# q and k of later sequences turned by VectorE, natural token order, and stack loads per head group

## The chip, the core and the metric

One Trainium2 chip, one core of it. The time is microseconds (us) on the device, from one launch of the whole program; a kernel's time is the median of its runs. TensorE multiplies matrices, ScalarE applies functions, VectorE and GpSimd work element by element, SyncE's queue (SP) issues nearly all transfers.

## What is computed

One transformer layer in float32 over 8 sequences of 512 tokens, model width 128, 16 heads of 8 dimensions:

```python
x = x + attn(layernorm(x))   # q, k, v = x @ W + b; q, k, v each layer-normed per head (8 dims), scale, bias
                             # scores = q.k / sqrt(8); softmax over 512 keys; out = probs @ v; out @ Wo + bo
x = x + ffn(layernorm(x))    # (silu(x @ wg.T) * (x @ wu.T)) @ wd.T, hidden 384, integer weights / 127
```

## The kernel before

**Turns and units.** The program runs 8 turns, one for each sequence's attention; turns 2 to 5 are a hardware loop, the others are written out. A turn has 16 units, `u` 0 to 15: four heads (a head group, `g = u // 4`) against 128 keys (`kt = u % 4`). In a unit TensorE multiplies scores for four heads (L897, four matmuls on row strips of 32 partitions, from the stacks `kst` and `qst`), ScalarE takes the exponential in two instructions (L771, three heads and then the fourth), and TensorE multiplies the probabilities of the unit before by `v` (L912, `times_v`). The scores of the next unit may be written as soon as the first of the two exponentials is done, since the first three banks of `scores` are single.

**Side pieces.** All other matrix work of the layer is cut into pieces that TensorE does behind `times_v` of a unit. The table `SIDE` says which unit has which piece, and `BANK` which of the two PSUM banks of `side` it writes. In turn i the pieces are: `a_v` (v of sequence i+1), `a_rq` and `a_rk` (the normed q and k of i+1 transposed by TensorE), `b_Wo` (output projection of i-1), `e_q` and `e_k` (q and k of i+2), `b_x2T` (transposes of i-1), `b_g0` to `b_u2` (gate and up products of i-1, three each), `b_d0` and `b_d1` (down product). A piece waits until VectorE has read what its bank held before: `read_out` names the semaphore for each.

**VectorE.** Its instructions stand in one order written by hand in its `turn(i, phase)`: `centred*` (centring with bias out of `side`), `heads_normed` (qk_n), `affined` (scale and bias of q and k, into `qk_f`), `first_part` and `second_part` (q and k split into two float16 parts), `take_sums` (reads out the attention's sum `oacc`, after 8 units each), `divide`, `turn_heads` (onT, for `b_Wo`), `ln2_stats`, `ln2_apply` (x2n, for `b_x2T`), `copy_x2T`, `silu` (ga), `times_up` (hT), `result` (y). An engine works strictly in its order.

**ScalarE** does the exponentials and three tanh in a turn, behind the second exponential of the units in `TANH_AT`. **GpSimd** does in each turn, in this order: `norm_power` of i+2 (ve, rs; it waits for the statistics and for v_c), `v_squares` (v_sq), `residual` (x_bo), `norm_power` of i-1.

**Transfers.** The float16 parts go to a DRAM buffer (`store_parts`) and come back with rows spread out as the stacks, in two halves of two groups each (`load_stack`). For the first sequence, group 0 goes straight from SBUF to SBUF (`own_stack`), group 1 and the second half through DRAM.

## Time and profile before

| | |
|---|---|
| time, median of 3 runs | 330.37 us (330.34 to 330.46) |
| the profiled execution | 330.57 us, its span 328.8 us |
| busy: TensorE, ScalarE, VectorE, GpSimd | 297.1 (90%), 268.8 (82%), 238.7 (73%), 48.5 us (15%) |
| first exponential, last exponential's start | 24.7 us, 308.6 us |
| first exponential of turn 3, of turn 4 | 133.0 us, 168.4 us |
| mean granted TensorE clock | 0.995 |

The span is from the first to the last instruction of the profiled execution. A busy share is an average: it doesn't say who waits for whom in a unit. TensorE's weight loads overlap its matmuls.

### The profile page before, as it was taken

The numbers are of one execution on the slowest core, as the hardware profiler recorded it, in microseconds if no ns is written. First come the engines' busy times: TensorE is split into PE (matmuls) and PEld (weight loads), VectorE is DVE, ScalarE is ACT, GpSimd is POOL, SyncE is SP. The second block draws the span as 40 slices with busy tenths as digits, with TensorE's granted clock in tenths as the row PEclk, the third lists the DMA queues.
The fourth block names the chain that finished last, engine by engine and source line by source line (L and its number), as shares of the span: only waits on it lengthen the run. The fifth ranks groups of instructions, "written<-read, shape, count | busy, mean of one in ns | idle before, by whom it ended". The sixth has DMA issues, their size and how long they took to land.

```text
span 328.8 us, 10326 instructions
## 1 busy us (share of the span) xinstructions
PE 297.1 (90%) x4002; PEld 131.8 (40%) x4002; DVE 238.7 (73%) x631; ACT 268.8 (82%) x300; POOL 48.5 (15%) x93
## 2 busy tenths in 40 slices
PE   7877957899999999999999999999998998789996
PEld 7773311233243424352353325342432332222676
DVE  4998997358887797869786888689774856272365
ACT  4429949999989998889979998999889998999511
POOL 7610200041004100140004100410021010110020
PEclk9999989999999999999999999999999999999999
DMA  6534140210325023401422032302320243000000
GB/s 187 161 112 142 34 160 4 80 54 0 101 96 163 2 78 119 139 20 64 127 87 73 0 119 85 116 0 96 96 99 2 66 130 131 2 0 2 34 3 32
DMA packets 21716, 24.76 MB, mean 75 GB/s; under 512 B 2096, under 2 KB 17712, under 8 KB 21680
## 3 DMA queue, kind: packets, MB, share of 16 engines
q1 hardware_dynamic: 21104, 23.59, 22.7%
q10 hardware_dynamic: 576, 0.69, 0.7%
q8 instruction: 23, 0.38, 0.5%
q14 instruction: 13, 0.11, 0.1%
HBM read 15.36 MB, written 8.65 MB: 73 GB/s over the span
## 4 chain that ended last, share of the span: by engine, by line
PE 48%; ACT 26%; issue 13%; DVE 9%; DMA 2%; POOL 1%; ACTq 1%; SPq 0%; POOLq 0%; DVEq 0%
ACT probs L771 25%; PE oacc L912 19%; PE side L844 14%; PE scores L897 9%; PE side L837 3%; DMA y<-in_x 2%; DVE qk_c L1090 1%; PE scores L998 1%; DVE x2n L1074 1%; ACT th L737 1%; PE scores L798 1%; POOL rs L591 1%; PE side L998 1%; DVE stats L1065 0%; DVE sums_t L1256 0%
## 5 line engine op out<-in xcount | busy, mean ns | idle before, releaser
L771 ACT ACTIVATE probs<-scores 128x1536 f32<-128x1536 f32 (+1 forms) x256 | 248.5, 1025 | 31.4 <-PE scores L897 28.3
L912 PE MATMUL oacc<-probs,vaug 128*32 128x512 f32 x1024 | 137.8, 610 | 9.0 <-DVE sums_t L1256 4.0
L897 PE MATMUL scores<-qst,kst 32*128 32x512 f16 x512 | 50.8, 386 | 13.5 <-ACT probs L771 11.2
L897 PEld LDWEIGHTS scores<-qst,kst 32*128 32x128 f16 x512 | 13.0, 91 | 67.7 <-ACT probs L771 58.3
L912 PEld LDWEIGHTS oacc<-probs,vaug 128*32 128x32 f32 x1024 | 20.4, 108 | 42.9 <-ACT probs L771 32.4
L589 POOL TENSOR_SCALAR ve<-mv 128x4 f32<-128x4 f32 (+1 forms) x17 | 4.0, 235 | 222.2 <-DVE mv L1068 190.9
L844 PE MATMUL side<-x2T_parts,gu_parts 128*32 128x512 f16 x504 | 34.9, 379 | 0.8 <-DVE x2T_parts L1296 0.5
L844 PEld LDWEIGHTS side<-x2T_parts,gu_parts 128*32 128x32 f16 x504 | 14.1, 96 | 32.6 <-issue 18.4
L844 PEld LDWEIGHTS side<-wqkv,xT 128*32 128x32 f32 x736 | 20.9, 110 | 12.5 <-issue 11.5
L844 PE MATMUL side<-wqkv,xT 128*32 128x128 f32 x736 | 24.1, 273 | 0.9 <-DMA xT<-in_xT 0.9
L1302 DVE SCALAR_TENSOR_TENSOR ga<-th,side 128x512 f32<-128x512 f32 x21 | 14.4, 685 | 12.1 <-ACT th L737 12.0
L844 PEld LDWEIGHTS side<-wdT,hT 128*32 128x32 f32 x672 | 18.9, 110 | 8.4 <-issue 6.3
L1309 DVE TENSOR_TENSOR hT<-side,ga 128x512 f32<-128x512 f32 x23 | 15.9, 690 | 7.1 <-PE side L844 6.2
L844 PE MATMUL side<-wdT,hT 128*32 128x128 f32 x672 | 20.9, 273 | 0.0
L798 PE MATMUL scores<-ident 128*128 128x128 f32 x126 | 17.3, 295 | 1.8 <-POOL ident L568 1.8
L1090 DVE SCALAR_TENSOR_TENSOR qk_c<-side,rs,wqkv 128x128 f32<-128x128 f32 x64 | 17.7, 343 | 1.7 <-PE side L844 1.0
L798 PEld LDWEIGHTS scores<-ident 128*128 128x128 f32 x126 | 16.1, 207 | 3.0 <-POOL ident L568 1.8
L591 POOL TENSOR_TENSOR rs<-ve,neg_half 128x4 f32<-128x4 f32 (+1 forms) x17 | 16.9, 997 | 1.4
L1284 DVE TENSOR_TENSOR x<-side,x_bo 128x512 f32<-128x512 f32 x7 | 4.8, 692 | 15.2 <-PE side L844 15.2
L1247 DVE TENSOR_TENSOR vaug<-v_c,hy 128x128 f32<-128x128 f32 x32 | 7.9, 287 | 9.4 <-PE oacc L912 9.3
L1074 DVE TENSOR_SCALAR x2n<-x,mv,rs 128x128 f32<-128x128 f32 x32 | 10.0, 371 | 5.1 <-POOL rs L591 5.0
L737 ACT ACTIVATE th<-side 128x512 f32<-128x512 f32 x21 | 12.6, 602 | 0.7
(161 smaller groups left out, 291.0 us busy)
## 6 DMA issues: line engine op xcount, KB each, us to landing
parts_dram<-parts SPq DMA_DIRECT2D x16, 256.0 KB, 2.5
qst<-parts_dram SPq DMA_DIRECT2D x15, 256.0 KB, 2.7
kst<-parts_dram SPq DMA_DIRECT2D x15, 256.0 KB, 3.1
x_res<-in_x SPq DMA_DIRECT2D x8, 256.0 KB, 3.5
parts_dram<-parts SPq DMA_DIRECT2D x16, 128.0 KB, 1.9
x_in<-in_x SPq DMA_DIRECT2D x7, 256.0 KB, 2.6
xT<-in_xT SPq DMA_DIRECT2D x7, 256.0 KB, 3.1
out_dram<-y SPq DMA_DIRECT2D x7, 256.0 KB, 2.1
```

The costliest lines, as they stand in the source:

```text
L591: pool.tensor_tensor(out=rs[:, ts], in0=ve[:, ts], in1=neg_half[:, ts], op=ALU.pow).then_inc(rs_done, 1)
L737: act.activation(th[:, j, :], gate, ACT.Tanh, scale=0.5 * GU_SCALE).then_inc(tanh_done, 1)
L771: act.activation(out, src, ACT.Exp).then_inc(exp_done, 1)
L798: pe.matmul(out, ident[:, :], ident[:, :], start=True, stop=True)
L837: last = pe.transpose(dst[:, k * P:(k + 1) * P], src(t), ident[:, :])
L844: last = pe.matmul(out[cols, :], weights[:, cols], moving, start=start, stop=stop)
L897: last = pe.matmul(scores[:, j if j < TRIPLE else TRIPLE + u % 2, :], kst[r, g, kt * P:(kt + 1) * P], qst[r, g, :], start=True, stop=True)
L912: last = pe.matmul(oacc[STRIP * j:STRIP * (j + 1), :], vaug[:, kt, NG * g + j, :], probs[:, kt, j, :], start=first, stop=last_of_half)
L1074: dve.tensor_scalar(dst[:, t, :], src[:, t, :], mv[:, t, 0:1], rs[:, t:t + 1], ALU.subtract, ALU.mult).then_inc(done, 1)
L1090: last = dve.scalar_tensor_tensor(out=out[:, t, :], in0=bank[:, t * D:(t + 1) * D], scalar=rs1[:, t:t + 1], in1=wqkv[:, bias, :], op0=ALU. ...
L1302: dve.scalar_tensor_tensor(out=ga[:, j, :], in0=th[:, j, :], scalar=1.0, in1=gate, op0=ALU.add, op1=ALU.mult)\
L1309: dve.tensor_tensor(out=hT[:, j, :], in0=up, in1=ga[:, j, :], op=ALU.mult)\
```

## The change

q and k of sequences 1 to 7 are no longer transposed by TensorE into PSUM: VectorE transposes 32x32 blocks from SBUF to SBUF (`turned`, into `qk_t`, written with a step of four elements) and `affined` reads that. Sequence 0 keeps TensorE's transposes. `a_rq` and `a_rk` leave the table, and the other pieces move to other units and banks; `b_g1` and `b_g2` share unit 11. Columns of q and k now stand in natural token order; the keys of a unit are therefore every fourth column of `kst`, and rows of the residual and the output are read and written as 512-byte pieces. Each stack load takes one group, in pieces of 256 bytes. All four groups of sequence 0 go from SBUF to SBUF. VectorE's order and `TANH_AT` change.

```diff
-SIDE = {0: ["a_v"], 1: ["a_rq"], 3: ["a_rk"], 4: ["b_Wo"], 5: ["e_q"], 6: ["e_k"], 7: ["b_x2T"],
-        8: ["b_g0"], 9: ["b_u0"], 10: ["b_g1"], 11: ["b_u1"], 12: ["b_g2"], 13: ["b_u2"], 14: ["b_d0"], 15: ["b_d1"]}
-BANK = {"a_v": 1, "a_rq": 0, "a_rk": 1, "b_Wo": 0, "e_q": 1, "e_k": 0, "b_x2T": 1, "b_g0": 1, "b_u0": 0, "b_g1": 1,
-        "b_g2": 1, "b_u1": 0, "b_u2": 0, "b_d0": 0}
-FIRST_SIDE = {1: ["a_v"], 5: ["a_rq"], 6: ["a_rk"], 7: ["e_q"], 8: ["e_k"]}
+SIDE = {0: ["a_v"], 3: ["b_Wo"], 4: ["e_q"], 5: ["e_k"], 6: ["b_x2T"], 9: ["b_g0"], 10: ["b_u0"], 11: ["b_g1",
+        "b_g2"], 12: ["b_u1"], 13: ["b_u2"], 14: ["b_d0"], 15: ["b_d1"]}
+BANK = {"a_v": 1, "b_Wo": 1, "e_q": 0, "e_k": 1, "b_x2T": 0, "b_g0": 1, "b_u0": 0, "b_g1": 1, "b_g2": 0,
+        "b_u1": 1, "b_u2": 1, "b_d0": 1}
+FIRST_SIDE = {1: ["a_v"], 7: ["e_q"], 8: ["e_k"]}
...
-                        eng.dma_start(stack[r:P:SLOTS, 0, :], parts[0:STRIP, part, which, :]).then_inc(group_loaded, 16)
+                        src = parts[STRIP * group:STRIP * (group + 1), part, which, :]
+                        eng.dma_start(stack[r:P:SLOTS, group, :], src).then_inc(loaded, 16)
...
-                for which, stack in ((0, qst), (1, kst)):
-                    src = parts_d[which].rearrange("(c q) r s -> (q r) c s", c=NG)
-                    sp.dma_start(stack[:, 2 * half:2 * half + 2, :], src[:, 2 * half:2 * half + 2, :])\
-                      .then_inc(loaded, 16)
+                for g in (2 * half, 2 * half + 1):
+                    for which, stack in ((0, qst), (1, kst)):
+                        src = parts_d[which].rearrange("a i s n c -> (i s) a n c")
+                        sp.dma_start(stack[:, g, :].rearrange("p (a c) -> p a c", c=P), src[:, :, g, :]).then_inc(loaded, 16)
...
+            for group in range(1, NG):
+                for part in range(2):
+                    for which, stack in ((0, qst), (1, kst)):
+                        own_stack(sp, which, part, stack, group, second_group_loaded if group == 1 else other_groups_loaded)
...
-            TANH_AT = {8: 0, 10: 1, 12: 2}
+            TANH_AT = {9: 0, 11: 1, 12: 2}
...
-                    last = pe.matmul(scores[:, j if j < TRIPLE else TRIPLE + u % 2, :], kst[r, g, kt * P:(kt + 1) * P],
+                    keys = kst[r, g, :].rearrange("p (c t) -> p t c", t=NT)
+                    last = pe.matmul(scores[:, j if j < TRIPLE else TRIPLE + u % 2, :], keys[:, kt, :],
...
+            def turned(b, w):
+                dve.wait_ge(qkn_done, 2 * b + w + 1)
+                at_least(dve, qkf_done, 2 * (b - 1) + w + 1)
+                dve.transpose(qk_t[:, w, :, :, :].rearrange("p n k t -> p n t k"), qk_n[:, w, :, :].rearrange("p t (n i) -> p n t i", i=STRIP))\
+                   .then_inc(qkt_done, 1)
+
             def affined(b, w):
-                dve.wait_ge(r_filled, 2 * b + w + 1)
+                dve.wait_ge(qkt_done, 2 * (b - 1) + w + 1)
                 sc, bi = ((q_aff[:, 0:1], q_aff[:, 1:2]), (k_aff[:, 0:1], k_aff[:, 1:2]))[w]
-                dve.tensor_scalar(qk_f[:, w, :], side[:, BANK[name], :], sc, bi, ALU.mult, ALU.add).then_inc(qkf_done, 1)
+                dve.tensor_scalar(qk_f[:, w, :], qk_t[:, w, :, :, :].rearrange("p n k t -> p (n k t)"), sc, bi,
+                                  ALU.mult, ALU.add).then_inc(qkf_done, 1)
...
             def first_part(b):
-                at_least(dve, parts_stored, 16 * PART_DMAS * b)
                 if isinstance(b, int) and b == 1:
                     dve.wait_ge(group_loaded, 16 * GROUP_DMAS)
+                    dve.wait_ge(second_group_loaded, 16 * OWN_DMAS)
+                    dve.wait_ge(other_groups_loaded, 32 * OWN_DMAS)
+                else:
+                    dve.wait_ge(parts_stored, 16 * PART_DMAS * (b - 1))
...
                     heads_normed(1)
-                    fill_v(0, 1)
-                    centred_v(1)
-                    ln1_stats(2)
+                    turned(1, 0)
+                    turned(1, 1)
                     affined(1, 0)
                     affined(1, 1)
                     first_part(1)
                     second_part(1)
+                    fill_v(0, 1)
+                    centred_v(1)
+                    ln1_stats(2)
+                    take_sums(0, 0)
                     centred(2, 0)
...
                     centred(2, 1)
                     later_square(2, 0)
                     later_square(2, 1)
-                    sums_v(1)
-                    take_sums(0, 0)
-                    divide(0, 0)
```

Three places in the instruction order of a turn follow, where the table and VectorE's order decide it.

TensorE, units 9 to 11 of turn 1 before: each gate or up product is 12 matmuls of L844 on `x2T_parts`, between a unit's `times_v` (L912) and the next unit's scores (L897).

```order
L844 MATMUL side<-x2T_parts,gu_parts 32x512 x12
L897 MATMUL scores<-qst,kst 128x512 x4
L912 MATMUL oacc<-probs,vaug 32x512 x4
L844 MATMUL side<-x2T_parts,gu_parts 32x512 x12
L897 MATMUL scores<-qst,kst 128x512 x4
```

The same place in the changed kernel, units 10 to 12 (there L839, L893 and L908 are the same lines):

```order
L839 MATMUL side<-x2T_parts,gu_parts 32x512 x12
L893 MATMUL scores<-qst,kst 128x512 x4
L908 MATMUL oacc<-probs,vaug 32x512 x4
L839 MATMUL side<-x2T_parts,gu_parts 32x512 x24
L893 MATMUL scores<-qst,kst 128x512 x4
L908 MATMUL oacc<-probs,vaug 32x512 x4
L839 MATMUL side<-x2T_parts,gu_parts 32x512 x12
```

Unit 11 now holds 24 matmuls in place of 12, and units 7 and 8 hold none.

VectorE, late in turn 1 before: `ga` is `silu` and `hT` is `times_up`, here of gates 1 and 2 (the last rows are the start of the head norm's inverse roots).

```order
L1302 SCALAR_TENSOR_TENSOR ga<-th,side 128x512
L1309 TENSOR_TENSOR hT<-side,ga 128x512
L1136 TENSOR_REDUCE qk_sum<-qk_sq 128x128
L1139 TENSOR_SCALAR hv<-qk_sum 128x128
L1302 SCALAR_TENSOR_TENSOR ga<-th,side 128x512
L1309 TENSOR_TENSOR hT<-side,ga 128x512
L1149 TENSOR_SCALAR hy<-hv 128x192
```

The same place in the changed kernel, from `times_up` of gate 0 on:

```order
L1319 TENSOR_TENSOR hT<-side,ga 128x512
L1136 TENSOR_REDUCE qk_sum<-qk_sq 128x128
L1139 TENSOR_SCALAR hv<-qk_sum 128x128
L1312 SCALAR_TENSOR_TENSOR ga<-th,side 128x512
L1274 RECIPROCAL rinv<-sums_t 128x32
L1278 TENSOR_TENSOR on_t<-sums_t,rinv 128x16x16
L1312 SCALAR_TENSOR_TENSOR ga<-th,side 128x512
L1319 TENSOR_TENSOR hT<-side,ga 128x512 x2
L1149 TENSOR_SCALAR hy<-hv 128x192
```

`times_up` of gate 1 has moved behind `silu` of gate 2, and `divide` of this turn's first half stands between the two `silu`.

VectorE at the start of turn 1 before:

```order
L1247 TENSOR_TENSOR vaug<-v_c,hy 128x4x4x8 x2
L1256 STREAM_TRANSPOSE sums_t<-oacc 128x512
L1090 SCALAR_TENSOR_TENSOR v_c<-side,rs,wqkv 128x128 x4
L1264 RECIPROCAL rinv<-sums_t 128x32
L1268 TENSOR_TENSOR on_t<-sums_t,rinv 128x16x16
L1065 BN_STATS stats<-x_in 128x6 x4
L1068 BN_AGGR mv<-stats 128x2 x4
L1205 TENSOR_SCALAR qk_f<-side,q_aff 128x512
L1278 STREAM_TRANSPOSE onT<-on_t 128x512
```

and in the changed kernel:

```order
L1065 BN_STATS stats<-x_in 128x6 x4
L1068 BN_AGGR mv<-stats 128x2 x4
L1266 STREAM_TRANSPOSE sums_t<-oacc 128x512
L1257 TENSOR_TENSOR vaug<-v_c,hy 128x4x4x8 x2
L1090 SCALAR_TENSOR_TENSOR v_c<-side,rs,wqkv 128x128 x4
L1204 STREAM_TRANSPOSE qk_t<-qk_n 128x4x4x32
L1210 TENSOR_SCALAR qk_f<-qk_t,q_aff 128x512
L1274 RECIPROCAL rinv<-sums_t 128x32
L1278 TENSOR_TENSOR on_t<-sums_t,rinv 128x16x16
L1288 STREAM_TRANSPOSE onT<-on_t 128x512
```

The statistics of the next x stand first now, and the new transpose and `affined` stand between v_c and the two instructions of `divide`.

## Rows read from the trace of the kernel before

**Rows 1.** Group of instructions: line, engine, names, count | busy us, mean ns | idle before:

```profile
L897 PEld LDWEIGHTS scores<-qst,kst 32*128 32x128 f16 x512 | 13.0, 91 | 67.7 <-ACT probs L771 58.3 <-issue 9.4
```

**Rows 2.** Timeline, turn 3, TensorE's scores: start, us, engine, line, [idle before, releaser]:

```profile
136.82 0.39 PE L897 MATMUL scores<-qst,kst 32*128 32x512 f16 x4
...
138.77 0.40 PE L897 MATMUL scores<-qst,kst 32*128 32x512 f16 x4 [0.47 <-ACT probs L771]
...
140.84 0.40 PE L897 MATMUL scores<-qst,kst 32*128 32x512 f16 x4
...
149.41 0.40 PE L897 MATMUL scores<-qst,kst 32*128 32x512 f16 x4
...
151.81 0.39 PE L897 MATMUL scores<-qst,kst 32*128 32x512 f16 x4
...
158.18 0.40 PE L897 MATMUL scores<-qst,kst 32*128 32x512 f16 x4
...
162.44 0.39 PE L897 MATMUL scores<-qst,kst 32*128 32x512 f16 x4
...
165.24 0.39 PE L897 MATMUL scores<-qst,kst 32*128 32x512 f16 x4
...
168.00 0.40 PE L897 MATMUL scores<-qst,kst 32*128 32x512 f16 x4
```

**Rows 3.** Timeline, the second half of turn 3:

```profile
151.04 0.83 PE L844 MATMUL side<-x2T_parts,gu_parts 128*32 128x512 f16 x12
...
152.13 1.07 PE L912 MATMUL oacc<-probs,vaug 128*32 128x512 f32 x8
...
161.08 0.69 DVE L1302 SCALAR_TENSOR_TENSOR ga<-th,side 128x512 f32<-128x512 f32 x1 [0.87 <-ACT th L737]
...
162.93 1.07 PE L912 MATMUL oacc<-probs,vaug 128*32 128x512 f32 x8
```

**Rows 4.** Timeline, VectorE and GpSimd early in turns 3 and 4:

```profile
136.86 0.87 DVE L1065 BATCH_NORM_STATS2 stats<-x_in 128x6 f32<-128x128 f32 x4
...
138.09 0.81 DVE L1205 TENSOR_SCALAR qk_f<-side,q_aff 128x512 f32<-128x512 f32 x1
...
138.44 0.23 POOL L589 TENSOR_SCALAR ve<-mv 128x4 f32<-128x4 f32 x1 [27.06 <-DVE mv L1068]
...
138.81 0.70 DVE L1278 STREAM_TRANSPOSE onT<-on_t 128x512 f32<-128x512 f32 x1
...
139.75 1.04 POOL L595 TENSOR_TENSOR v_sq<-v_c 128x512 f32<-128x512 f32 x1
...
168.01 0.69 DVE L1315 TENSOR_TENSOR y<-side,x 128x512 f32<-128x512 f32 x1 [0.39 <-PE side L844]
...
170.50 1.13 DVE L1090 SCALAR_TENSOR_TENSOR v_c<-side,rs,wqkv 128x128 f32<-128x128 f32 x4
...
171.55 0.35 DVE L1264 RECIPROCAL rinv<-sums_t 128x32 f32<-128x32 f32 x1
...
171.93 0.43 DVE L1268 TENSOR_TENSOR on_t<-sums_t,rinv 128x256 f32<-128x256 f32 x1
```

**Rows 5.** Timeline, the same two engines early in turn 6:

```profile
242.28 1.04 POOL L595 TENSOR_TENSOR v_sq<-v_c 128x512 f32<-128x512 f32 x1 [24.77 <-DVE v_c L1090]
...
242.50 1.11 DVE L1268 TENSOR_TENSOR on_t<-sums_t,rinv 128x256 f32<-128x256 f32 x1
```

**Rows 6.** Timeline, turn 0, with SyncE's queue (SPq):

```profile
19.01 2.30 SPq L421 DMA_DIRECT2D qst<-parts  x3
...
34.00 1.29 DVE L1196 TENSOR_TENSOR qk_n<-qk_c,hy 128x512 f32<-128x512 f32 x2
...
41.29 1.22 DVE L1233 TENSOR_TENSOR parts<-qk_f,parts 128x1024 f16<-128x1024 f32 x1
...
47.38 1.91 PE L912 MATMUL oacc<-probs,vaug 128*32 128x512 f32 x8 [3.66 <-DVE sums_t L1256]
...
49.94 13.47 ACT L771 ACTIVATE probs<-scores 128x1536 f32<-128x1536 f32 x13 [4.17 <-PE scores L897]
```

More of the change, by code:

```diff
@@ L69 @@
 WARM_LAST = {"on": 8, "x2n": 11, "x2T": 3}
[L70 removed]
+STACK_DMAS = NG
 W_KS = ([0], [1, 2])
@@ L130, in occupants_before @@
     if phase == "first":
-        p, turn = [(p, turn) for p, turn in PROLOGUE if same_bank(p) and (p, sequence_of(p, turn)) not in ELSEWHERE][-1]
+        p, turn = [(p, turn) for p, turn in PROLOGUE
+                   if (p, sequence_of(p, turn)) not in ELSEWHERE and same_bank(p)][-1]
         return [(p, sequence_of(p, turn))]
@@ L410, in build, with own_stack @@
         GROUP_DMAS = 2 * SLOTS
-        def own_stack(eng, which, part, stack):
+        OWN_DMAS = 2 * (SLOTS - 1)
+        def own_stack(eng, which, part, stack, group, loaded):
             if which == 0:
@@ L522, in _ @@
             for part in range(2):
-                own_stack(sp, 0, part, qst)
-            for part in range(2):
-                for which in range(2):
-                    own_store(sp, which, part)
-            for which, stack in ((0, qst), (1, kst)):
-                load_second_group(sp, which, stack)
+                own_stack(sp, 0, part, qst, 0, group_loaded)
+            for group in range(1, NG):
+                for part in range(2):
+                    for which, stack in ((0, qst), (1, kst)):
+                        own_stack(sp, which, part, stack, group, second_group_loaded if group == 1 else other_groups_loaded)
+            sp.wait_ge(shift_stored, 32)
             sp.wait_ge(flag_ready, 1)
@@ L1398, in turn @@
                     return
-                fill_v(i, 1)
+                if early:
+                    ln1_stats(i + 2)
                 if behind:
                     take_sums(i - 1, 1)
+                fill_v(i, 1)
                 if ahead:
                     centred_v(i + 1)
+                    turned(i + 1, 0)
+                    affined(i + 1, 0)
                 if behind:
                     divide(i - 1, 1)
-                if early:
-                    ln1_stats(i + 2)
+                    turn_heads(i - 1)
+                    ln2_stats(i - 1)
                 if ahead:
-                    affined(i + 1, 0)
-                if behind:
-                    turn_heads(i - 1)
-                if ahead:
-                    affined(i + 1, 1)
-                if behind:
-                    ln2_stats(i - 1)
+                    turned(i + 1, 1)
                 if early:
@@ L1419, in turn @@
                     ln2_apply(i - 1)
+                if ahead:
+                    affined(i + 1, 1)
+                if early:
+                    later_square(i + 2, 0)
+                if ahead:
+                    sums_v(i + 1)
                 if early:
@@ L1425, in turn @@
                 if early:
-                    later_square(i + 2, 0)
+                    later_square(i + 2, 1)
+                if behind:
+                    silu(i - 1, 0, side[:, BANK["b_g0"], :])
                 if ahead:
                     first_part(i + 1)
-                divide(i, 0)
-                if ahead:
-                    sums_v(i + 1)
-                if behind:
-                    silu(i - 1, 0, side[:, BANK["b_g0"], :])
-                if early:
-                    later_square(i + 2, 1)
+                    second_part(i + 1)
                 if behind:
                     times_up(i - 1, 0, side[:, BANK["b_u0"], :])
-                if ahead:
-                    second_part(i + 1)
-                if behind:
-                    silu(i - 1, 1, side[:, BANK["b_g1"], :])
-                    times_up(i - 1, 1, side[:, BANK["b_u1"], :])
                 if early:
@@ L1445, in turn @@
                 if behind:
+                    silu(i - 1, 1, side[:, BANK["b_g1"], :])
+                divide(i, 0)
+                if behind:
                     silu(i - 1, 2, side[:, BANK["b_g2"], :])
+                    times_up(i - 1, 1, side[:, BANK["b_u1"], :])
                     times_up(i - 1, 2, side[:, BANK["b_u2"], :])
@@ L1457, in turn @@
                     result(i - 1)
-                if ahead:
-                    fill_v(i + 1, 0)
             turn(0, "first")
```

101 lines of the change are left out of this document (51 added, 50 removed).

## The prediction

> **What bounds the kernel now.** I read the page first: TensorE is busy 90%, ScalarE 82%, VectorE 73%, and none is full, so I looked at one turn of the loop in the timeline, by the starts of its scores [rows 2]. Call s0 to s15 the starts of a turn's sixteen scores; a unit lasts from one to the next. Turn 3 gives: a unit without a side piece 138.77 - 136.82 = 1.95 (unit 2); with four full transposes of q or k 2.07 (unit 3); units 4 to 7 with Wo, e_q, e_k and x2T 8.57 together; unit 8 2.40; units 9 to 13, one gate or up product each, 162.44 - 151.81 = 10.63, so 2.13 each; unit 14, with half a down product, 2.80, and unit 15 2.76. The reader is to see two regimes: in a plain unit TensorE waits for ScalarE (the idle time named in the row of 138.77), and the two exponentials set 1.95; in a unit with a float32 piece TensorE itself is the longer. Every 0.1 us that TensorE starts a unit's scores late is lost for both. Unit 8 is 2.40 because its product waited for x2T_parts: the product starts at 151.04 [rows 3], 1.63 after the unit's start, where otherwise a piece follows the scores by 0.32 and 1.07 of `times_v` [rows 3]. Turn 0 has one large hole: `times_v` of unit 8 waits 3.66 us for `take_sums` on VectorE, and ScalarE stands idle 4.17 us [rows 6].
>
> **Turn 0: a gain of about 4.1.** `take_sums(0, 0)` moves ahead of the centring of sequence 2, its squares and sums_v. What stays ahead of it is what VectorE did from 34.00 to 42.51 [rows 6] (qk_n's start to the end of the second part), plus two block transposes at 0.70 [rows 4] (that of onT). The transposes put its start at 43.9 at worst, and at about 42.3 if the waits in that stretch go (`affined` no longer waits for TensorE, and the first of `parts` doesn't meet v_sq any more, below). It takes about 0.7, and `times_v` wants it at 47.38 - 3.66 = 43.72. So the hole shrinks by 3.3 to 4.2; I take 4.1. `first_part(1)` now also waits until 18 more small transfers have read `parts`: three took the queue 2.30 [rows 6], so 18 at most 13.8, issued by 35.1, landed before 38, when VectorE gets there. xT of sequence 2, queued behind them, has until unit 7 at about 40.
>
> **Transposes off TensorE: -0.2 a turn.** Two units lose theirs. One was worth 2.07 - 1.95 = 0.12; the other stood behind a longer unit and I take 0.07.
>
> **x2T earlier: -0.45 a turn.** x2T is now in unit 6 and the first product in unit 9, so 2.40 becomes 1.95, provided VectorE has copied x2T by then. By my count of its order it has, with over 1 us to spare.
>
> **Two products in unit 11: +0.67 a turn.** A product is busy 0.83 [rows 3]; directly behind another part of its filling is hidden, so I take 0.67 (bounds 0.6 and 0.83): unit 11 becomes 2.80. Five product units become four plus this.
>
> **The new wait, for u2: +0.85 a turn.** Both u1 and u2 write bank 1, so u2 waits until `times_up` has read u1, and in VectorE's order that stands behind `silu` of gate 2, which waits for the tanh at the end of unit 12. Before, this `silu` started at 161.08 [rows 3], 2.90 after s12 at 158.18 [rows 2]. It takes 0.69, `times_up` about the same again, and with 0.1 for the signal u2 starts at s12 + 4.4 at the latest and 4.3 at the earliest. From a product's start to the next scores is 151.81 - 151.04 = 0.77, so s14 comes at s12 + 5.1 where it was 162.44 - 158.18 = 4.26: +0.85. Unit 14 gives 0.17 back: its `times_v` had to wait for the exponentials (162.93 - 162.44 = 0.49 against 152.13 - 151.81 = 0.32 [rows 2, 3]) and won't. So the late part of the turn costs 0.67 + 0.85 - 0.17 = +1.35, the early part gives 0.64: **+0.7 a turn**, in seven turns (the last has the same second half) **+5.0**. The same chain then runs on: the inverse roots, `fill_v` and `heads_normed` now all stand ahead of `result`, so y starts about 0.3 later than 168.01 [rows 4].
>
> **The start of the turn: 0 to +0.6 in six turns.** Measured from s0 (168.00 in turn 4). y at 0.3, to the next instruction 0.6; the statistics 138.09 - 136.86 = 1.23 [rows 4]; sums and vaug 1.05; so v_c starts at 3.2 and ends at 4.3. The transpose 0.70; `affined` reads SBUF now: no row has it at this shape, from PSUM it took 0.81 [rows 4], half of that is the lower bound, I take 0.5. The reciprocal 171.93 - 171.55 = 0.38, so on_t starts at about 5.9. GpSimd meanwhile waits for v_c, since the statistics are early: ve at 4.4, and v_sq 139.75 - 138.44 = 1.31 later [rows 4], 5.7 to 6.75. In turn 6 on_t started 0.22 after v_sq, took 1.11 in place of 0.43 and ended 0.29 after v_sq's end [rows 4, 5]. The same here would end on_t at 7.05, onT at 7.8, and Wo starts at 7.9. TensorE would start it at 7.3: unit 0 at 2.2 (a_v is a piece like Wo, e_q and e_k: 8.57 less about 2.0 for x2T, over three), two plain units 3.9, then 1.2 for scores and `times_v`. So Wo and all behind it come 0.6 late: 3.6 in turns 1 to 6. If on_t slips in before v_sq, it costs nothing (onT at 7.1). The two are 0.2 apart on a sum of eight terms, so I take half, **+1.8**.
>
> **The keys' step and the block transposes' step.** The weight loads of the scores take 91 ns [rows 1] and stand in the chain from one exponential to the next in plain units. No row shows one with a step; I take no change, bounded above by doubling, 0.09 in each of 128 units, 11.6. The new transpose writes with a step of 16 bytes; lower bound 0.70, upper twice that. The second case is cheap: ahead of on_t it hides in the hold above, ahead of x2T's copy in the spare time, about 1.5 in all. In the page "SBUF — State Buffer", section "Door 1: The DMA port swizzle", the Trainium skill says that accesses reach full bandwidth with at least two hits on a 16-byte line. By that rule the keys, 8 bytes apart, load as before, and the transposes' writes, each in a new line, would be dearer, which speaks against this change; no row here compares the two.
>
> **Transfers: 0.** A stack half is now four transfers. The parts are stored earlier than before, and the loads were issued at the end of a turn with a quarter of a turn to spare. The 512-byte pieces of the residual and the output are hidden the same way, except the last store, 0.1.
>
> **Sum.** -4.1 + 5.0 + 1.8 = +2.7, on the profiled execution's 330.57, which stands 0.2 over the median: 333.3 there, **333.1** for the median of the runs.
>
> **The rivals.** (1) *The forecast* holds with on_t between free and always held: 331.3 to 334.9. 0.52. (2) *Faster*: the wait for u2 isn't paid. It would need u1 read out before u2's turn; the place is VectorE between `silu` of gates 1 and 2, and it decides if the tanh of gate 2 ran more than about 0.8 earlier against s12 than in the rows. Then units 12 to 14 are as before, unit 11's 0.67 and the early gain cancel, turns keep their length, and turn 0's gain stands alone: 330.37 - 4.1 = 326.3. For it speaks that I lay out an order by hand, against it that tanh stands behind the second exponential in both. 0.28, with all smaller mixtures that end below 329.7. (3) *Weight loads with a step*: half the bound is +5.8 on the forecast, 338.9; the point from which it decides is 0.02 a unit. 0.10. (4) *Turn 0's hole only moves*: the first parts or a slow transpose keep `take_sums` late and 2 of the 4.1 are lost: 335.1. 0.10.
>
> **How the numbers follow.** A measurement of this kernel can tell about 0.2%, 0.66 us, from no change. Faster is rival 2, and a little of the forecast's lower edge: 0.30. Same, 329.7 to 331.0, lies between rival 2 and the forecast with on_t free: 0.13. The rest is slower: 0.57. The range, 326.2 to 336.5, holds the forecast, most of rival 2 and rival 4; the forecast's own range is 331.3 to 334.9.
>
> **What would show it.** In the changed kernel: in turn 0 TensorE's wait for sums_t under 1 us; plain units still at 1.95 (if not, the weight loads); unit 11 at 2.80; in unit 13 a TensorE wait of about 0.9 for VectorE's hT, each turn; on_t at 1.1 rather than 0.43 beside v_sq, and Wo's piece late by half a microsecond; turns of 36.1 to 36.7, from first exponential to first exponential, where turn 3 had 168.4 - 133.0 = 35.4. The prediction is wrong if u2 finds its bank free, or if some piece that I count as in time (x2T, a_v behind y, `times_v` of unit 8) is late.

## The result and the profile after

The changed kernel takes **341.17 us** (340.95 to 341.37, 4 runs) where the kernel before took 330.36 beside it: ratio 1.0326, 95% interval 1.0304 to 1.0347. It is slower, as forecast, but by 10.8 us where the forecast said 2.7, and it lies outside the range. The line numbers of the changed kernel are 4 or 5 lower on TensorE and ScalarE, those of VectorE from L1204 on 10 higher: scores L893, `times_v` L908, side pieces L839, exponentials L766.

The page, beside the table of before: TensorE's busy time fell by 4.8 us although the span grew by 10.7.

```profile
span 339.5 us, 10249 instructions
...
PE 292.3 (86%) x3946; PEld 127.4 (38%) x3946; DVE 252.4 (74%) x645; ACT 270.0 (80%) x300; POOL 49.3 (15%) x93
```

Turn 3 in the timeline, TensorE's scores, as in [rows 2] (start, us, engine, line):

```profile
134.88 0.41 PE L893 MATMUL scores<-qst,kst 32*128 32x512 f16 x4
...
137.27 0.41 PE L893 MATMUL scores<-qst,kst 32*128 32x512 f16 x4
...
139.23 0.41 PE L893 MATMUL scores<-qst,kst 32*128 32x512 f16 x4
...
141.19 0.41 PE L893 MATMUL scores<-qst,kst 32*128 32x512 f16 x4 [0.41 <-ACT probs L766]
...
144.36 0.41 PE L893 MATMUL scores<-qst,kst 32*128 32x512 f16 x4
...
161.76 0.41 PE L893 MATMUL scores<-qst,kst 32*128 32x512 f16 x4
...
166.78 0.41 PE L893 MATMUL scores<-qst,kst 32*128 32x512 f16 x4
...
169.43 0.41 PE L893 MATMUL scores<-qst,kst 32*128 32x512 f16 x4
...
172.17 0.41 PE L893 MATMUL scores<-qst,kst 32*128 32x512 f16 x4
```

A turn now has 172.17 - 134.88 = 37.3 us where it had 35.4. Unit by unit, from one start to the next:

```
turn 3, unit   0    1    2    3    4    5    6    7    8    9    10   11   12   13   14   15
before        2.20 2.02 1.94 2.07 2.23 2.20 2.20 1.95 2.40 2.11 2.13 2.13 2.13 2.13 2.80 2.76
after         2.38 1.96 1.96 3.17 2.22 2.21 1.96 1.96 1.97 2.21 2.10 2.78 1.99 3.03 2.65 2.73
```

The last seven units are 17.49 against 16.19, so +1.30, and unit 3 alone is 1.10 longer. All turns together, from the starts of their first scores (the last one to its last exponential):

```
turn      0      1      2      3      4      5      6      7
before  37.18  35.77  35.37  35.39  35.35  35.26  35.37  35.19
after   33.95  37.16  38.83  37.28  37.31  37.20  36.81  36.26
```

Turn 0 gives 3.23, the others lose 1.1 to 2.0 each and turn 2 loses 3.46; with 0.65 more ahead of the first scores that makes 10.6 of the span's 10.7. Two questions stood open after this view: what makes unit 3 so long (the forecast had 2.2 or 2.8 there), and what is special in turn 2.

VectorE and GpSimd early in turn 3, with TensorE's Wo piece behind them (these answer to [rows 4, 5]; L1204 is the new transpose, L1278 on_t, L1288 onT):

```profile
139.44 1.25 DVE L1204 STREAM_TRANSPOSE qk_t<-qk_n 128x512 f32<-128x512 f32 x1
...
140.72 0.55 DVE L1210 TENSOR_SCALAR qk_f<-qk_t,q_aff 128x512 f32<-128x512 f32 x1
...
141.03 1.13 POOL L591 TENSOR_TENSOR v_sq<-v_c 128x512 f32<-128x512 f32 x1
...
141.57 0.88 DVE L1278 TENSOR_TENSOR on_t<-sums_t,rinv 128x256 f32<-128x256 f32 x1
...
142.48 0.71 DVE L1288 STREAM_TRANSPOSE onT<-on_t 128x512 f32<-128x512 f32 x1
...
143.34 1.08 PE L839 MATMUL side<-wo,onT 128*32 128x128 f32 x32 [0.60 <-DVE onT L1288]
```

The reader is to see two things. The transpose takes 1.25 us where onT, of the same shape and without a step, takes 0.71. And on_t takes 0.88, ending 0.29 after v_sq's end (142.45 against 142.16), which is the forecast's mechanism to the hundredth. TensorE waits 0.60 for onT. In turns 1 to 5 it is on_t that is held so, in turn 6 `affined` (1.59).

The late part of the turn, VectorE's silu and times_up with TensorE's products (as [rows 3]):

```profile
160.35 1.48 PE L839 MATMUL side<-x2T_parts,gu_parts 128*32 128x512 f16 x24
...
164.68 0.69 DVE L1312 SCALAR_TENSOR_TENSOR ga<-th,side 128x512 f32<-128x512 f32 x1 [1.20 <-ACT th L733]
165.28 0.68 DVE L1319 TENSOR_TENSOR hT<-side,ga 128x512 f32<-128x512 f32 x1
...
166.02 0.83 PE L839 MATMUL side<-x2T_parts,gu_parts 128*32 128x512 f16 x12 [0.75 <-DVE hT L1319]
```

The two products of unit 11 take 1.48, and the product u2 waits 0.75 for hT, behind a ga that waits 1.20 for the third tanh. And turn 2, where VectorE stands still 1.51 us inside the four aggregations of the statistics, with nothing in the profile that it waits for ("issue"):

```profile
97.82 0.23 DVE L1068 BATCH_NORM_AGGREGATE mv<-stats 128x2 f32<-128x6 f32 x2
...
99.56 0.40 DVE L1068 BATCH_NORM_AGGREGATE mv<-stats 128x2 f32<-128x6 f32 x2 [1.51 <-issue]
...
100.78 1.06 PE L908 MATMUL oacc<-probs,vaug 128*32 128x512 f32 x8 [1.98 <-ACT probs L766]
```

This is the first pass through the hardware loop's body. In the kernel before `fill_v` and `take_sums` stood first in a turn; now the statistics do, and `take_sums`, which frees the place that `times_v` of unit 1 writes, is queued behind the stall. `take_sums` ends at 100.73, and `times_v` starts at 100.78; the exponential that the last row names had been done before.

### The profile page after: what moved, and what is told of

It is laid out like the page before. It is cut to its first block and busy times, and to the rows that moved or that the text cites. A ratio compares the mean times of both kernels' runs of the same rounds, so it can differ in the third digit from the quotient of the medians.

```text
span 339.5 us, 10249 instructions
## 1 busy us (share of the span) xinstructions
PE 292.3 (86%) x3946; PEld 127.4 (38%) x3946; DVE 252.4 (74%) x645; ACT 270.0 (80%) x300; POOL 49.3 (15%) x93
## 5 line engine op out<-in xcount | busy, mean ns | idle before, releaser
L766 ACT ACTIVATE probs<-scores 128x1536 f32<-128x1536 f32 (+1 forms) x256 | 248.4, 1024 | 41.5 <-PE scores L893 38.6
L908 PE MATMUL oacc<-probs,vaug 128*32 128x512 f32 x1024 | 136.3, 604 | 8.0 <-ACT probs L766 2.1
L893 PE MATMUL scores<-qst,kst 32*128 32x512 f16 x512 | 52.8, 402 | 21.7 <-ACT probs L766 20.9
L893 PEld LDWEIGHTS scores<-qst,kst 32*128 32x128 f16 x512 | 15.3, 108 | 87.4 <-ACT probs L766 76.2
L839 PE MATMUL side<-x2T_parts,gu_parts 128*32 128x512 f16 x504 | 33.6, 380 | 5.2 <-DVE hT L1319 5.2
L908 PEld LDWEIGHTS oacc<-probs,vaug 128*32 128x32 f32 x1024 | 20.2, 108 | 41.6 <-ACT probs L766 27.0
L839 PEld LDWEIGHTS side<-x2T_parts,gu_parts 128*32 128x32 f16 x504 | 13.7, 96 | 34.5 <-issue 13.2
L839 PEld LDWEIGHTS side<-wqkv,xT 128*32 128x32 f32 x736 | 20.2, 110 | 13.9 <-issue 11.0
L839 PE MATMUL side<-wqkv,xT 128*32 128x128 f32 x736 | 24.1, 273 | 1.0 <-DVE qk_c L1090 0.6
L839 PEld LDWEIGHTS side<-wdT,hT 128*32 128x32 f32 x672 | 19.0, 110 | 8.3 <-issue 4.8
L839 PE MATMUL side<-wdT,hT 128*32 128x128 f32 x672 | 20.9, 273 | 0.0
L793 PE MATMUL scores<-ident 128*128 128x128 f32 x126 | 18.6, 309 | 1.8 <-POOL ident L564 1.8
L1266 DVE STREAM_TRANSPOSE sums_t<-oacc 128x512 f32<-128x512 f32 (+1 forms) x17 | 11.6, 683 | 10.4 <-PE oacc L908 10.2
L793 PEld LDWEIGHTS scores<-ident 128*128 128x128 f32 x126 | 17.6, 224 | 3.0 <-POOL ident L564 1.8
L587 POOL TENSOR_TENSOR rs<-ve,neg_half 128x4 f32<-128x4 f32 (+1 forms) x17 | 18.0, 1058 | 1.4
L1204 DVE STREAM_TRANSPOSE qk_t<-qk_n 128x512 f32<-128x512 f32 x14 | 16.5, 1193 | 0.0
L598 POOL TENSOR_TENSOR x_bo<-x_res,bo_row 128x512 f32<-128x512 f32 x8 | 11.1, 1390 | 22.1 <-DMA x_res<-in_x 22.1
```

The lines of the kernel that those rows point to most:

```text
L587: pool.tensor_tensor(out=rs[:, ts], in0=ve[:, ts], in1=neg_half[:, ts], op=ALU.pow).then_inc(rs_done, 1)
L598: pool.tensor_tensor(out=x_bo[:, :, :], in0=x_res[:, :, :], in1=bo2_row[:, :].unsqueeze(1).broadcast_to((P, NT, D)), op=ALU.add)\
L766: act.activation(out, src, ACT.Exp).then_inc(exp_done, 1)
L793: pe.matmul(out, ident[:, :], ident[:, :], start=True, stop=True)
L839: last = pe.matmul(out[cols, :], weights[:, cols], moving, start=start, stop=stop)
L893: last = pe.matmul(scores[:, j if j < TRIPLE else TRIPLE + u % 2, :], keys[:, kt, :], qst[r, g, :], start=True, stop=True)
```

## The experiments

Each edit is made in the changed kernel unless it says otherwise. "Less" is the difference of the medians to the changed kernel's 341.17. The kernel before, which ran beside every one of them, moved by up to 0.5 between these occasions (329.99 to 330.48), so the ratios are the better measure: by them experiments 1, 2, 5 and 7 gave 4.3, 4.4, 1.0 and 7.6.

**1. times_up of gate 1 ahead of silu of gate 2.** Theory: the new wait for u2 comes from this order alone.

```diff
-                    silu(i - 1, 2, side[:, BANK["b_g2"], :])
                     times_up(i - 1, 1, side[:, BANK["b_u1"], :])
+                    silu(i - 1, 2, side[:, BANK["b_g2"], :])
```

> The changed kernel with one edit: on VectorE times_up of gate 1 stands ahead of silu of gate 2, as before the change. Theory (the wait for u2 costs what it shows): the trace of the changed kernel has s12 to s14 at 1.99 + 3.03 = 5.02 in turn 3 where it was 4.26, so units 12 and 13 should fall to about 4.25, unit 14 rise by about 0.15, net 0.6 to 0.8 in each of seven turns: 336.0 to 337.0 from 341.2. Rival (the wait hides a later one, such as the down product waiting for hT of gate 2): TensorE's wait moves to unit 14 and the time stays within 1 us of 341.2.

336.56 us, ratio 1.0196 (1.0178 to 1.0215): 4.6 less. Turn 3, TensorE and VectorE around unit 13:

```profile
162.02 0.69 DVE L1319 TENSOR_TENSOR hT<-side,ga 128x512 f32<-128x512 f32 x1 [0.39 <-PE side L839]
...
162.83 0.69 DVE L1312 SCALAR_TENSOR_TENSOR ga<-th,side 128x512 f32<-128x512 f32 x1
163.25 0.83 PE L839 MATMUL side<-x2T_parts,gu_parts 128*32 128x512 f16 x12
```

hT now stands ahead of ga and u2 starts with no wait beyond its place; unit 13 is 2.29 instead of 3.03, unit 14 2.80 instead of 2.65. The wait for u2 and what it costs are shown: 4.1 in units 13 and 14 of seven turns. Another 0.45 went in unit 0, since y is no longer late (in turn 3 it starts 0.03 after the turn's first scores, where it was 0.35).

**2. The transpose written without a step.** This changes the order of the output's columns, so part of what is computed is not the reference's; the work is the same.

```diff
-    dve.transpose(qk_t[:, w, :, :, :].rearrange("p n k t -> p n t k"), ...)
+    dve.transpose(qk_t[:, w, :, :, :].rearrange("p n k t -> p (n k t)")
+                  .rearrange("p (n t k) -> p n t k", t=NT, k=STRIP), ...)
```

> The changed kernel with VectorE's transposes written without a step, so that the columns of q and k of sequences 1 to 7 come out in another order (the output is not the reference's). Theory A (the step of 16 bytes makes a transpose dear): 1.2 us falls to 0.70. Theory B (at the turn's start on_t is held by GpSimd's v_sq in any case, so the dearer transpose is hidden there): Wo's piece comes as late as before within 0.1, and the time falls by less than 1 us, 340.2 to 341.2. If the transpose itself makes Wo late, the time falls by 0.5 in six turns, to about 338.2.

336.19 us, ratio 1.0192 (1.0162 to 1.0223): 5.0 less. Groups of instructions of this kernel and then the same two of the changed one (busy us, mean ns):

```profile
L1204 DVE STREAM_TRANSPOSE qk_t<-qk_n 128x512 f32<-128x512 f32 x14 | 9.8, 703 | 0.0
...
L1278 DVE TENSOR_TENSOR on_t<-sums_t,rinv 128x256 f32<-128x256 f32 (+1 forms) x17 | 7.6, 450 | 0.6
```

```profile
L1204 DVE STREAM_TRANSPOSE qk_t<-qk_n 128x512 f32<-128x512 f32 x14 | 16.5, 1193 | 0.0
...
L1278 DVE TENSOR_TENSOR on_t<-sums_t,rinv 128x256 f32<-128x256 f32 (+1 forms) x17 | 9.7, 569 | 0.6
```

Its timeline in turn 3:

```profile
139.08 0.42 DVE L1278 TENSOR_TENSOR on_t<-sums_t,rinv 128x256 f32<-128x256 f32 x1
139.09 1.31 POOL L591 TENSOR_TENSOR v_sq<-v_c 128x512 f32<-128x512 f32 x1
...
139.54 0.71 DVE L1288 STREAM_TRANSPOSE onT<-on_t 128x512 f32<-128x512 f32 x1
```

The step costs 0.49 us of VectorE for each transpose. But the second effect is as large: on_t starts 6.13 after the turn's first scores where it was 6.69, and v_sq stays (6.14, it was 6.15). So on_t starts 0.01 ahead of v_sq, takes 0.42, and it is GpSimd that is held (1.31). Unit 3 falls to 2.36 in every turn, 4.3 in turns 1 to 6 together. So the dear transpose and the hold don't overlap, they add: the one causes the other.

**3. GpSimd's order turned round.** x_bo first in a turn, as soon as its data is there, v_sq last, behind both `norm_power`.

```diff
+                if "b" in PHASES[phase]:
+                    residual(i - 1)
                 ...
-                if "a" in PHASES[phase]:
-                    v_squares(i + 1)
                 ...
-                    residual(i - 1)
+                if "a" in PHASES[phase]:
+                    v_squares(i + 1)
```

> The changed kernel with GpSimd's order in a turn changed: x_bo first, then norm_power of i+2, norm_power of i-1, and v_sq last, so that nothing long of GpSimd runs beside on_t. Theory (the hold): on_t falls from 0.88 to 0.43 in turn 3 and Wo's piece comes 0.45 earlier in turns 1 to 6, minus what x2n loses beside v_sq, up to 0.4: 338.5 to 341.0. Rival (the hold is a coincidence of the record): on_t stays at 0.88 and the time at 341.2.

342.35 us, ratio 1.0377 (1.0355 to 1.0399): slower. The timeline shows where the hold went (L1171 is the last step of the inverse roots, hy):

```profile
131.48 1.35 POOL L598 TENSOR_TENSOR x_bo<-x_res,bo_row 128x512 f32<-128x512 f32 x1 [21.16 <-DMA x_res<-in_x]
...
131.72 1.33 DVE L1171 SCALAR_TENSOR_TENSOR hy<-ht,hy 128x192 f32<-128x192 f32 x1
...
135.79 1.08 PE L840 MATMUL side<-wqkv,xT 128*32 128x128 f32 x32 [0.91 <-DVE y L1326]
```

on_t takes 0.42 again and unit 3 fell to 2.68 to 2.87 in the loop, but now hy, which takes 0.36 alone, is held to 1.33 beside x_bo, y comes late, and the piece a_v waits 0.91 for y: unit 0 grows from 2.3 to 3.3. A hold that is moved needs a place where VectorE has time.

**4. The heads turned before q.** `turned` and `affined` of q behind `turn_heads`.

```diff
-                    turned(i + 1, 0)
-                    affined(i + 1, 0)
                 if behind:
                     divide(i - 1, 1)
                     turn_heads(i - 1)
-                    ln2_stats(i - 1)
+                if ahead:
+                    turned(i + 1, 0)
+                    affined(i + 1, 0)
+                if behind:
+                    ln2_stats(i - 1)
```

> The changed kernel with the first turned and affined of a turn behind turn_heads, so that divide and turn_heads follow v_c at once, as before the change. Theory (late onT makes unit 3 long): unit 3 falls from 3.17 to 2.2 in turns 2 to 5 and less in 1 and 6; 5.0 us in all, 336 to 337. Rival (the work ahead of x2T's copy is the next to be late): half of it comes back as a wait for x2T_parts or sums_t at units 8 and 9, 338 to 340.

337.50 us, ratio 1.0216 (1.0195 to 1.0238): 3.7 less. Timeline, turn 3:

```profile
140.51 1.03 POOL L591 TENSOR_TENSOR v_sq<-v_c 128x512 f32<-128x512 f32 x1
...
141.47 1.61 DVE L1210 TENSOR_SCALAR qk_f<-qk_t,q_aff 128x512 f32<-128x512 f32 x1
141.51 1.28 POOL L598 TENSOR_TENSOR x_bo<-x_res,bo_row 128x512 f32<-128x512 f32 x1
```

Unit 3 is 2.36. The hold now falls on `affined`, 1.61 in place of 0.55, ending 0.29 after x_bo's end, where nobody waits. The gain stays under experiment 2's 5.0 because turn 2 lost more: its unit 1 grew from 3.39 to 4.10.

**5. The keys side by side.** `kst` read without the step of four; a unit's probabilities then meet the rows of v of other keys, so the attention is not the reference's; the work is the same.

```diff
-                    keys = kst[r, g, :].rearrange("p (c t) -> p t c", t=NT)
+                    keys = kst[r, g, :].rearrange("p (t c) -> p t c", t=NT)
```

> The changed kernel with each unit's keys taken as 128 adjacent columns of kst again, so that keys and values of a unit don't belong together (the output is not the reference's). Theory (the step of the keys costs in every unit): the weight load falls from 108 to 91 ns, plain units from 1.96 and 2.02 to 1.94 and 2.00, and the time by 0.02 in each of 128 units, 2 to 2.5 us: about 338.9. Rival (the load is hidden): below 0.7 us.

339.48 us, ratio 1.0296 (1.0269 to 1.0323): 1.7 less. The group of the scores' weight loads, of the changed kernel and then of this one (it answers to [rows 1]):

```profile
L893 PEld LDWEIGHTS scores<-qst,kst 32*128 32x128 f16 x512 | 15.3, 108 | 87.4 <-ACT probs L766 76.2 <-issue 11.1
```

```profile
L893 PEld LDWEIGHTS scores<-qst,kst 32*128 32x128 f16 x512 | 13.0, 90 | 87.0 <-ACT probs L766 76.5 <-issue 10.4
```

A step of 8 bytes costs 18 ns a load and 0.01 to 0.02 in a plain unit (1.96 and 2.02 against 1.94 or 1.95 and 2.00). What that makes in all is less sure than it looks: the turns are 1.1 shorter in sum, the ratios give 1.0, and the two ratios' intervals overlap. (In the profiled run the first scores are also 0.8 earlier, which is no effect of the edit: q's norm ahead of them starts 0.67 earlier, and the clock has 0.13, see the last section.) The price is about 0.01 in each of 128 units.

**6. The kernel before, with turn 0's early sums alone.**

```diff
+                    take_sums(0, 0)
+                    divide(0, 0)
                     centred(2, 0)
                     ...
                     sums_v(1)
-                    take_sums(0, 0)
-                    divide(0, 0)
```

> The kernel before, with take_sums and divide of turn 0 moved ahead of the centring of sequence 2, nothing else. Theory (turn 0's hole is VectorE's order alone): unit 9 of turn 0 falls from 5.90 to about 2.1, 3.5 to 4.1 us: 326.1 to 326.9. Rival (the hole only moves, since the parts of sequence 1 and the centring of sequence 2 are late for turn 1): 328 to 330.

**326.11 us**, ratio 0.9893 (0.9865 to 0.9921). Unit 9 of turn 0 falls from 5.90 to 2.01 and the turn from 37.18 to 33.08: the forecast's 4.1. This one move of the change is worth 1.1%, and beats both kernels.

**7. One product a unit, from unit 8.** The banks, the tanh places and VectorE's late order of the kernel before, the rest as changed.

```diff
-SIDE = {..., 6: ["b_x2T"], 9: ["b_g0"], 10: ["b_u0"], 11: ["b_g1", "b_g2"], 12: ["b_u1"], 13: ["b_u2"], ...}
+SIDE = {..., 6: ["b_x2T"], 8: ["b_g0"], 9: ["b_u0"], 10: ["b_g1"], 11: ["b_u1"], 12: ["b_g2"], 13: ["b_u2"], ...}
-            TANH_AT = {9: 0, 11: 1, 12: 2}
+            TANH_AT = {8: 0, 10: 1, 12: 2}
```

> The changed kernel with the six products one to a unit from unit 8 on, with the banks, the tanh and VectorE's silu and times_up order of before; x2T stays in unit 6. Theory: the double product (0.65) and the wait for u2 (0.7 after unit 14's give-back) go, and so does a_v's wait behind y (0.15), since the down product is in the other bank: 1.4 to 1.5 in each of seven turns, 330.5 to 331.5 from 341.2. Rival (x2T's copy isn't done when unit 8 wants it): unit 8 grows by 0.3 to 0.5, 333 to 335.

333.32 us, ratio 1.0096 (1.0072 to 1.0121): 7.9 less, not down to 331.5. Turn 3 is 36.20, with units 8 to 13 at 2.13 to 2.16 and no wait for a bank, but unit 3 at 3.28: the early part keeps its price when the late part is mended. The turns gained 1.0 to 1.3 each and not 1.4 to 1.5. The expectation had left out that unit 8 now has a product (2.13 for 1.96) and that unit 12 is no longer the short one behind two products (2.13 for 1.99).

**8. The sums ahead of the statistics.**

```diff
-                if early:
-                    ln1_stats(i + 2)
                 if behind:
                     take_sums(i - 1, 1)
+                if early:
+                    ln1_stats(i + 2)
```

> The changed kernel with one edit: the sums of a head group are taken (take_sums) ahead of the statistics of the later sequence in VectorE's order, so that the stall of 1.5 us at the loop's first pass stands behind the sums. Theory: unit 1 of turn 2 falls from 3.39 to 1.96 us, the other turns stay, and the time falls by 1.0 to 1.4 us to about 340 us. Rival: the stall moves along with whatever is first, and the time does not change by more than 0.5 us.

343.41 us, ratio 1.0393 (1.0357 to 1.0429): **2.2 slower**, a miss. Unit 1 of turn 2 did fall to 1.96. But the statistics had filled a time in which VectorE waits for the sums anyway (turn 3, VectorE):

```profile
137.91 0.72 DVE L1266 STREAM_TRANSPOSE sums_t<-oacc 128x512 f32<-128x512 f32 x1 [0.57 <-PE oacc L908]
...
138.55 0.83 DVE L1065 BATCH_NORM_STATS2 stats<-x_in 128x6 f32<-128x128 f32 x4
...
140.37 1.13 DVE L1090 SCALAR_TENSOR_TENSOR v_c<-side,rs,wqkv 128x128 f32<-128x128 f32 x4
```

The transpose of the sums waits 0.57 for TensorE, and v_c starts 140.37 - 136.33 = 4.04 after the turn's start where it was 138.40 - 134.88 = 3.52. So Wo is 0.5 later: unit 3 is 3.7 in turns 3 to 5. In turn 1 it is 4.58 and unit 4 2.88, and there the granted clock fell. These are two stretches of turn 1: from and to, length in us, then the busy time and instructions of TensorE, its weight loads, VectorE, ScalarE and GpSimd, and as the third number from the end the granted clock of TensorE as a share:

```profile
66.00:67.50 1.50, 0.37 (x4) 0.00 (x1) 1.35 (x2) 1.27 (x2) 1.50 (x2) 1.00 0.00 0
67.50:70.00 2.50, 2.47 (x40) 1.68 (x44) 0.48 (x1) 0.00 (x0) 0.27 (x1) 0.50 0.00 0
```

After 1.5 us in which TensorE worked 0.37, the granted clock was 0.50 (1.2 in place of 2.4 GHz) for 2.5 us. The kernel before shows 0.50 from 48 to 50 us too, right behind the hole of turn 0, and experiment 6 shows 1.00 there, which is part of what closing that hole gives.

**9. Two banks exchanged in turn 0.**

```diff
-BANK.update({"f_q": BANK["e_q"], "f_k": BANK["e_k"]})
+BANK.update({"f_q": BANK["e_k"], "f_k": BANK["e_q"]})
...
                 name, sem_f = (("e_q", q_filled), ("e_k", k_filled))[w]
+                if isinstance(b, int) and b == 1:
+                    name = ("f_q", "f_k")[w]
```

> The changed kernel with one edit: the two banks that hold the first half of q and k of sequence 1 in turn 0 are exchanged, so that the bank which the second product of a.v wants in unit 1 comes free earlier. Theory: unit 1 of turn 0 falls from 3.2 to 2.5 us, and the time by 0.7 us to about 340.5 us. Rival: the other bank's reader is as late, and nothing changes.

340.07 us, ratio 1.0297 (1.0280 to 1.0315): 1.1 less. Unit 1 of turn 0 is 2.41 where it was 3.18, and in the profile that is what the edit gives: 0.8. The first product of v for sequence 1 writes bank 1; before, what stood in bank 1 there was q, which VectorE centres first; the new table had made it k, centred second.

**10. GpSimd waits for onT.** x_bo and v_sq, in this order, wait until `turn_heads` is done.

```diff
                 if "b" in PHASES[phase]:
+                    pool.wait_ge(onT_done, i)
+                    residual(i - 1)
                 ...
-                if "b" in PHASES[phase]:
-                    residual(i - 1)
```

> The changed kernel with one edit: GpSimd's x_bo and v_sq (in this order) wait until the last block transpose of the output (onT) is done, so that neither runs beside VectorE's on_t. What is left in unit 3 is then the block transpose of q or k at 1.2 us by itself. Theory: on_t takes 0.43 us instead of 0.88, unit 3 is 2.75 us in turns 2 to 5 (3.2 before) and 2.0 to 2.7 in the others, and the time falls by 0.45 us in five turns to about 338.8 us. Rival A: the transposes are all of it and unit 3 stays at 3.2 us. Rival B: the hold is all of it and unit 3 falls to 2.36 us.

338.40 us, ratio 1.0241 (1.0219 to 1.0262): 2.8 less. Timeline, turn 3:

```profile
140.65 0.43 DVE L1280 TENSOR_TENSOR on_t<-sums_t,rinv 128x256 f32<-128x256 f32 x1
...
141.97 1.08 PE L841 MATMUL side<-wo,onT 128*32 128x128 f32 x32 [0.24 <-DVE onT L1290]
142.07 1.28 POOL L598 TENSOR_TENSOR x_bo<-x_res,bo_row 128x512 f32<-128x512 f32 x1 [1.67 <-DVE onT L1290]
```

on_t takes 0.43 and unit 3 is 2.81 to 2.86: of the 3.17 to 3.32 in the loop the hold is 0.36 to 0.49, and the step, 0.49 of VectorE, is the 0.45 left over experiment 2's 2.36. Both rivals, that one of them is all of it, fall in the loop. In turns 1 and 6 unit 3 goes to 2.36 already: there the dear transpose by itself costs nothing.

**11. All mends together**: 4, 7, 8 and 9 in one kernel. It holds the edit of 8 too, which by itself cost time.

```diff
+SIDE = {..., 8: ["b_g0"], 9: ["b_u0"], 10: ["b_g1"], 11: ["b_u1"], 12: ["b_g2"], 13: ["b_u2"], ...}
+BANK.update({"f_q": BANK["e_k"], "f_k": BANK["e_q"]})
...
                     take_sums(i - 1, 1)
+                if early:
+                    ln1_stats(i + 2)
...
                     turn_heads(i - 1)
+                if ahead:
+                    turned(i + 1, 0)
+                    affined(i + 1, 0)
```

> The changed kernel with all found so far: products apart as in e7, turned and affined behind turn_heads, take_sums ahead of the statistics, and the banks of sequence 1's q and k exchanged so that a_v of turn 0 follows the first half of the centring. The output is the reference's. Theory: per turn 35.0 to 35.2 (2.21 + 4 x 1.96 + 6.66 + 2.12 + 10.65 + 5.5), and turn 0 at 33.3: 324.5 to 326.5, faster than before. Rival (VectorE is too full, a wait comes back at units 8 or 9): 327 to 330.

329.37 us, ratio 0.9979 (0.9968 to 0.9990, 10 runs): the rival's range, not the theory's. Turn 3 is 35.74 and turn 0 33.32. Unit 3 is 2.36, but unit 8 is 2.54. Timeline, turn 3, the second part of x2T and the first product:

```profile
148.66 0.69 DVE L1308 SCALAR_TENSOR_TENSOR x2T_parts<-side,x2T_parts 128x512 f16<-128x512 f32 x1
...
149.50 0.83 PE L839 MATMUL side<-x2T_parts,gu_parts 128*32 128x512 f16 x12 [0.23 <-DVE x2T_parts L1308]
```

VectorE, with two transposes of 1.2 more in the turn's first half, isn't through with x2T when unit 8 wants it. But the transposes alone aren't shown to be the reason. In experiment 4, which has them too, x2T's second part ends 18.11 after the turn's first scores, here 18.62; v_c starts at 3.50 there and 4.04 here, and that is the edit of 8. No run has 4, 7 and 9 without 8, so what they are worth stays open.

**12. The kernel before with 6 and its side pieces spread.**

```diff
-SIDE = {0: ["a_v"], 1: ["a_rq"], 3: ["a_rk"], 4: ["b_Wo"], 5: ["e_q"], 6: ["e_k"], 7: ["b_x2T"],
+SIDE = {0: ["a_v"], 1: ["a_rq"], 2: ["a_rk"], 3: ["b_Wo"], 4: ["e_q"], 5: ["e_k"], 6: ["b_x2T"],
```

> The kernel before with the two edits that the runs point to: turn 0's sums and quotients ahead of the centring of the later sequences, and the side products of a turn spread so that the product of x2 stands by itself. Theory: unit 8 falls from 2.40 to 2.13 us in each turn, and the time to 324.0 to 324.8 us (326.1 with the first edit alone). Rival: unit 3 or 6 grows by as much as unit 8 falls, and the time stays at 326 to 327 us.

**325.34 us**, ratio 0.9856 (0.9839 to 0.9872). Unit 8 fell to 2.13 as expected, unit 2 with unit 3 grew by 0.3 and units 10 and 11 by 0.06, and units 4 to 7 together fell by 0.27; turn 3 is 35.21 where experiment 6 has 35.41. That is between the two cases, some 0.9 less than experiment 6 by the turns; the two intervals overlap, so that it is better than 6 rests on the profile and not on the times.

## Why the prediction was right in sign and wrong in size

**Right: the late part.** +1.35 a turn was forecast, +1.30 is there: unit 11 at 2.78 (2.80), units 12 and 13 5.02 (5.1), unit 14 giving back 0.15 (0.17), and experiment 1 takes the wait away, 4.1 us in units 13 and 14 of seven turns. Rival 2, that this wait isn't paid, fell.

**Right: turn 0's hole.** Experiment 6 shows 4.1 us by itself. The changed kernel kept only 3.2, because of a cost beside it: a_v's bank in turn 0 (experiment 9, 0.8 us in that turn). I had looked at who writes a bank next in the loop's table, not in `FIRST_SIDE`. This is the forecast's own last warning, "some piece that I count as in time" is late. Rival 4 had a loss there too, but of 2 and from a late `take_sums`, which is not what happened.

**Wrong, the step that failed: "The second case is cheap: ahead of on_t it hides in the hold above, ahead of x2T's copy in the spare time, about 1.5 in all".** I bounded the transpose from above at twice 0.70 and it came to 1.19, within the bounds. What failed was the claim that it hides. I had put on_t 0.2 from slipping in before v_sq, taken half the hold, and then let a dearer transpose cost nothing. But GpSimd waits for v_c, which stands *ahead* of the transpose, and on_t stands behind it: every 0.1 that the transpose grows moves on_t towards v_sq and v_sq not at all. It first turns "half held" into "always held", and then adds itself, since TensorE waits for the end of the chain. Experiments 2, 4 and 10 show it from three sides. In unit 3 of turns 1 to 6 there is 4.3 less without the step and 2.45 less with the hold alone gone, and with both off the path unit 3 is 2.36. Forecast for the two together were 1.8; so 2.5 of the 8.1 missed are here.

**Wrong in smaller terms.** Counted by the starts of the scores, measured less forecast, the miss is 0.65 ahead of the first scores, 0.9 in turn 0, 6.6 in units 0 to 8 of turns 1 to 7, and -0.2 in their units 9 to 15: 7.9 of the 8.1.

Of the 6.6, the step above has 2.5 and turn 2's stall, which wasn't in the sum, 1.4. A free Wo in unit 3 was counted at 2.2; behind a plain unit it is 2.36 (experiment 2), because `times_v` there waits for the exponential, the same 0.15 that I gave back at unit 14: 0.9 in six turns. a_v behind the later y makes unit 0 longer, 0.6 in six turns; the forecast named this as a sign of being wrong and gave it no price, and experiment 1 takes 0.45 of it back. The keys' step was put at no change and costs 0.8 in these units and 1.1 in all turns (experiment 5). I had written the point from which it decides as 0.02 a unit, and it is 0.01, so rival 3 is real at a fifth of its size. And turn 7 had no transposes to be spared: 0.2. Together 6.4; 0.2 stay open.

The 0.9 in turn 0 is the bank above. Of the 0.65 ahead of the first scores, 0.54 belong to the change: see the last section.

**The rule of the 16-byte lines, and the lock.** In "SBUF — State Buffer", section "Door 1: The DMA port swizzle", the Trainium skill has accesses at full bandwidth with two or more on a 16-byte line. The transposes' writes, one on a line, agree: 1193 against 703 ns. The keys, two on a line, don't quite: 108 against 90 ns. ScalarE's float16 write of the last section, two on a line as well, doesn't at all: 1.50 against 0.78 us. I had let this rule speak against the change and then given it no time, since I held the dear case hidden. In the same page of the Trainium skill, section "Who interferes with whom", contention between VectorE and GpSimd is a lock that the first takes for its whole instruction; the trace agrees (on_t ending 0.29 after v_sq's end, and in experiment 2 v_sq held when on_t starts 0.01 ahead).

**What stays open.** Why VectorE stands 1.5 us in the loop's first pass. It stands in turn 2 alone, inside the aggregations, in each of the eleven kernels that have the new transposes. Its length goes from 0.22 (experiment 8, sums first) to 1.62 (experiment 4), but its end lies 3.3 to 3.6 us after the turn's first scores in all of them, whatever VectorE did before. In the kernel before, VectorE is busy there and shows no stall. So it looks like something with a time of its own that VectorE waits for; what it is, no run settled.

## What to carry to other kernels

When two engines leave one common start and collide later, price the chain of each from that start: a cost that stands on only one of them isn't hidden by the collision, it decides who wins it, and may be paid twice. A lower busy time of the fullest engine (4.8 us here) says nothing while the units are set by waits; ask of each moved piece who reads its bank last, in the written-out first turn too. Try each part of a large change alone: here one move of two lines was worth more than the whole, and its gain was buried under the rest.
